# One visit for the adapter matmul pairs of a routed body's second and third tile, with the other engines' tile work in another order

## Reference

```python
x = x + tanh(g_xattn[0]) * ssm(ctx_1024, layernorm(x))      # scan over DI = 512 channels x DS = 16 states
x = x + tanh(g_ffn[0]) * moe(layernorm(x))
# ssm, per step of the scan:
state = state * exp(d_t * A) + (d_t * u_t) * B_t
y_t = einsum('ben,bn->be', state, C_t)
# moe: F = 8 experts, K = 8 sub-experts each, R = 8 (adapter rank), I = 352
def _fused_linear(x, W, qa, qb, scale, w):
    out = x @ W.T
    a = einsum('th,krh->tkr', x, qa)
    b = einsum('tkr,khr->tkh', a, qb)
    return out + scale * einsum('tkh,tk->th', b, w)
def expert(..., w):
    xe = x + w @ muW.T
    gate = silu(_fused_linear(xe, gW, gqa, gqb, gs, w))
    up = _fused_linear(xe, uW, uqa, uqb, us, w)
    return _fused_linear(gate * up, dW, dqa, dqb, ds, w)
# y = sum over experts of their output times a routing weight, plus a shared expert of width 704
```

## Time and profile before

| | us |
|---|---|
| median of 3 runs (lowest, highest) | 1700.19 (1699.39, 1701.23) |
| the profiled execution's own time | 1701.69 |
| its span, first to last instruction | 1699.9 |
| busy: TensorE, its weight loads | 1576.4 (93%), 1161.0 (68%) |
| busy: DVE, ACT, POOL | 1166.0 (69%), 617.0 (36%), 727.1 (43%) |

### The profile page before, as it was taken

How to read it: one execution, slowest core, us unless ns; L and a number is a source line. 1 busy time by engine, 2 the same in 40 slices (tenths; PEclk the granted TensorE clock), 3 DMA queues, 4 the chain that set the end, 5 groups by cost and what they waited for, 6 DMA issues and landing times.

```text
span 1699.9 us, 19507 instructions
## 1 busy us (share of the span) xinstructions
PE 1576.4 (93%) x6856; PEld 1161.0 (68%) x6856; DVE 1166.0 (69%) x1638; ACT 617.0 (36%) x971; POOL 727.1 (43%) x522
## 2 busy tenths in 40 slices
PE   3788798798889999999999999999999999999999
PEld 2434476466666678767777777777777777777776
DVE  5798864598999976488888755688888653333333
ACT  4555344444454433433433243433433221111111
POOL 2377322389798811067777401287687000000000
PEclk8799899799999999999999999999999999999999
DMA  3555735887878755757567545577665456566552
GB/s 132 155 199 191 268 108 190 273 324 279 282 279 287 264 216 190 250 204 254 204 222 257 184 160 199 182 283 235 241 243 180 151 210 218 169 225 216 199 186 84
DMA packets 109888, 365.15 MB, mean 215 GB/s; under 512 B 20000, under 2 KB 45600, under 8 KB 94048
## 3 DMA queue, kind: packets, MB, share of 16 engines
q1 hardware_dynamic: 100320, 330.09, 55.9%
q10 hardware_dynamic: 9472, 33.82, 5.8%
HBM read 293.62 MB, written 70.25 MB: 214 GB/s over the span
## 4 chain that ended last, share of the span: by engine, by line
PE 62%; DVE 21%; issue 6%; ACT 5%; DMA 3%; POOL 2%; SPq 1%; ACTq 0%; DVEq 0%; POOLq 0%
PE b_g L690 14%; PE b_u L690 13%; PE b_u L781 7%; DVE ring L1441 5%; PE b_q L781 3%; PE b_g L781 3%; PE b_q L736 3%; DVE ring L1447 3%; PE b_g L754 3%; PE b_g L721 2%; DVE tt L1415 2%; PE b_g L714 2%; DVE xx L1415 1%; PE b_d L675 1%; DVE z L1415 1%
## 5 line engine op out<-in xcount | busy, mean ns | idle before, releaser
L1338 POOL TENSOR_TENSOR ring<-du,rep 128x512 f32<-128x512 f32 x256 | 346.6, 1357 | 172.6 <-DVE du L1519 90.7
L690 PE MATMUL b_g<-xnb,gm 128*128 128x512 f32 (+1 forms) x1440 | 360.2, 399 | 6.1 <-DVE tt L1415 5.3
L690 PE MATMUL b_u<-xnb,gm 128*128 128x512 f32 (+1 forms) x1440 | 349.2, 391 | 0.0
L690 PEld LDWEIGHTS b_g<-xnb,gm 128*128 128x128 f32 (+1 forms) x1440 | 254.6, 181 | 95.9 <-issue 30.2
L1441 DVE TENSOR_TENSOR_SCAN ring<-b_a,ring 128x512 f32<-128x512 f32 x256 | 311.0, 1215 | 10.3 <-POOL ring L1338 7.0
L1347 POOL TENSOR_TENSOR yx<-yx,ring 128x512 f32<-128x512 f32 x192 | 261.2, 1361 | 130.8 <-DVE ring L1447 130.4
L690 PEld LDWEIGHTS b_u<-xnb,gm 128*128 128x128 f32 (+1 forms) x1440 | 257.4, 179 | 71.2
L1415 DVE SCALAR_TENSOR_TENSOR tt<-tt,b_g 128x512 f32<-128x512 f32 (+1 forms) x120 | 82.0, 684 | 235.8 <-ACT tt L918 235.6
L918 ACT ACTIVATE b_a<-delta,a_neg 128x512 f32<-128x512 f32 x256 | 173.4, 681 | 120.0 <-DVE ring L1441 118.8
L781 PE MATMUL b_u<-dwt,hhl 128*128 128x512 f32 (+1 forms) x720 | 187.0, 396 | 0.4 <-DVE hhl L1418 0.4
L918 ACT ACTIVATE tt<-b_g 128x512 f32<-128x512 f32 (+1 forms) x120 | 71.1, 593 | 308.7 <-PE b_u L721 281.3
(11 more groups left out here) (231 smaller groups left out, 2117.9 us busy)
## 6 DMA issues: line engine op xcount, KB each, us to landing
gm<-scr_gm SPq DMA_DIRECT2D x60, 1024.0 KB, 7.8
dwt<-scr_dw SPq DMA_DIRECT2D x30, 1536.0 KB, 6.7
rep<-bc_d ACTq DMA_DIRECT2D x64, 512.0 KB, 5.0
gm<-scr_gm SPq DMA_DIRECT2D x30, 768.0 KB, 4.5
dqt<-scr_dq SPq DMA_DIRECT2D x24, 896.0 KB, 9.1
scr_gm<-gm SPq DMA_DIRECT2D x20, 1024.0 KB, 7.3
scr_dw<-dwt SPq DMA_DIRECT2D x10, 1536.0 KB, 6.2
qat<-scr_qa SPq DMA_DIRECT2D x24, 512.0 KB, 10.5
```

Source lines behind the costliest of these rows:

```text
L690: i = mm(out_b[0:IW[m], :], w, v, start=(n == 0), stop=(n == 11 and not is_routed(s)))
L1338: v.tensor_tensor(ring[:, T % NRING], du[:, T % 4, :], rep[:, N % NREP, 0], ALU.mult).then_inc(pool_dbu, 1)
```

## The change

TensorE does up and gate of the third tile before the second tile's adapters, and then both tiles' adapter pairs one after the other. The other engines' orders follow: ScalarE does tanh of the second and third tile one after the other, behind the slot c, and what stood between them (`h_hi` of the second, `root`, `hi("gm1")`, and in e = 0 `d_u` and the first exp) goes ahead of both or behind them. VectorE does slot c before `hidden` of the second tile, and `gate_z` of the second kind too. The tiles of h1 and c change places so that they stay in order of T. Instructions are neither added nor removed.

```diff
-            return {"a": (t0, t0 + 1), "h0": (t0 + 2,), "b": (t0 + 3,), "h1": (t0 + 4,), "c": (t0 + 5,),
+            return {"a": (t0, t0 + 1), "h0": (t0 + 2,), "b": (t0 + 3,), "c": (t0 + 4,), "h1": (t0 + 5,),
                     "h2": (t0 + 6,), "d": (t0 + 7,), "e": (t0 + 8,), "f": (t0 + 9,)}[slot]
...
# TensorE, routed
                 up(s, 1, 1)
-                adapters(s, 1).then_inc(pe_gu, 1)
                 up_waits(s, 2)
                 up(s, 2, 0)
                 up(s, 2, 1)
+                adapters(s, 1).then_inc(pe_gu, 1)
                 adapters(s, 2).then_inc(pe_gu, 1)
...
# ScalarE, routed
-                tanh(s, 1)
-                slot("h1")
-                h_hi(s, 1)
                 if more and e == 0:
                     d_u(nb, range(HC))
                     exp_tile(nb, 0)
                 if more and e == 4:
                     tanh_z(nb, 1)
                 if more and e == 5:
                     tanh_z(nb, 3)
+                slot("c")
+                tanh(s, 1)
+                tanh(s, 2)
+                slot("h1")
+                h_hi(s, 1)
+                if more and e == NF - 1:
+                    root(2 * nb + 1)
+                slot("h2")
+                h_hi(s, 2)
                 if split_next:
                     hi("gm1", s + 1)
-                slot("c")
-                if more and e == NF - 1:
-                    root(2 * nb + 1)
-                tanh(s, 2)
-                slot("h2")
-                h_hi(s, 2)
...
# VectorE, routed
-                hidden(s, 1, mid("h1"))
-                slot("c")
                 if more and e == 4:
                     gate_z(nb, 1)
                 if more and e == 5:
                     gate_z(nb, 3)
+                slot("c")
+                hidden(s, 1, mid("h1"))
                 if more and e == NF - 1:
                     variances(2 * nb + 1)
                     scales(2 * nb + 1, False)
```

## The result

The changed kernel takes 1731.58 us (median of 4 runs, 1730.29 to 1733.01) against 1700.31 for the kernel before, timed beside it (4 runs, 1699.39 to 1701.23). The ratio is 1.0182, with a 95% interval of 1.0166 to 1.0198. The forecast was slower, by 15.2 us; it is slower by 31, outside the range of 1703 to 1726.

The account below looks back on a forecast made before the run. TensorE bounds b = 1 to 3, VectorE (nearly GpSimd) b = 0. Terms: b = 0 +5.6, b = 1 and 2 +11.0, b = 3 -1.4, together +15.2 on 1701.7; median 1715.4 us, range 1703 to 1726.

Parts of the forecast that it names:

- The merged visit's saving: TensorE, routed bodies: one entry and exit of the adapter visit goes in each, 0.43 us.
- The width: TensorE's step from 128-column to 96-column pairs: taken as 0.23 like others; as a mode change, 10 us worse.
- Hidden and adapter_a in b = 1 and 2: TensorE waits at adapter_a for the third tile's late hl: +1.1 in e = 2, 6; -0.25 in e = 1, 5.
- e = 4: b = 1, 2: c_copy and shared zt delay the hiddens; less a wait already there, +0.85 each.
- e = 7: No qa fills the gap, work between hiddens delays norm_x1: +3.6 in b = 1, 2, +3.0 in b = 0; b = 3 +1.6.
- b = 0, e = 1 to 6: VectorE-bound bodies: GpSimd stands at lo_piece until hi("gm1"), now behind the third tile's rounding; +4.5 in all.
- The chain from the end of VectorE's h of the third tile: b = 0, e = 1: hi ends about 376.6, piece 2.37, two tile steps of 1.3; scan input at 381.6, not 381.29.
- The next thing in GpSimd's queue: b = 0, e = 1 to 6: GpSimd work behind the scan's input, for which the forecast's sum has no term.
- The rest of the new orders in b = 0: e = 1 to 6: two gate_z back to back cost 0.75 in e = 4, 5; e = 2 gets 1.3 back.
- The rival of a jam in GpSimd: b = 0: GpSimd's delay stays from body to body, +10 and not +4.5; 1721 to 1728 us; 9%.
- e = 0: Third tile's tanh comes earlier, so TensorE reaches adapter_a sooner: -0.8 each in b = 1, 2, -1.9 in b = 0.
- The rival of the clock: Waits in e = 7 lower TensorE's clock, adding about 1.7 to 3 us each time; 1720 to 1726 us; 6%.

Follow-up runs that it names:

- experiment 6: Changed kernel, but in e = 2, 4 and 6 only c_copy stands behind the third tile's rounding on ScalarE; 1721.63 us, ratio 1.0124.
- Experiment 4: Changed kernel, but in e = 7 variances, scales (VectorE) and root (ScalarE) stand ahead of both tiles' hidden and tanh; 1729.03 us, ratio 1.0161.
- experiment 1: Changed kernel, but ScalarE rounds gm1 behind the second tile's rounding again, ahead of slot h2; 1712.6 us, ratio 1.0071.
- experiment 2: Kernel before, but ScalarE's rounding of gm1 moved behind the third tile's rounding; 1716.4 us, ratio 1.0085.
- experiment 3: Changed kernel, but in e = 0 ScalarE does both tanh ahead of the scan's first exp; 1724.34 us, ratio 1.0131.
- all_four: Changed kernel with gm1's rounding back, both tanh first in e = 0, variances, scales, root first in e = 7, c_copy behind the rounding; 1690.95 us, ratio 0.9944.

## Why the prediction was right in direction and wrong in size

**The merged visit's saving** (0.43) measured 0.35 in b = 3. The width costs nothing that shows. The Trainium skill (TensorEngine Tiling (Array Packing), Key Properties) says that changing the tiling mode, and not just the tile, drains the engine. The trace agrees so far as the step from 128 to 96 columns, 0.23 like the others, shows no gap.

**Hidden and adapter_a in b = 1 and 2** (+1.1 in e = 2 and 6, -0.25 in e = 1 and 5, +0.1 in e = 3): +1.2, -0.23, -0.03. The chain worked out from the earlier trace rows held, and experiment 6 took `c_copy`'s part away. e = 4 was put at +0.85 and measured +0.4.

**e = 7** (+3.6, +3.6, +3.0, and +1.6 in b = 3): +3.8, +3.6, +3.0, +1.7. Experiment 4 shows that 2.4 and 2.1 of it in b = 1 and 2 is the work between the two hiddens, as I had said.

**The step that failed: b = 0, e = 1 to 6**, "+0.4 in odd e, about +1.2 where c_copy holds the rounding too", +4.5 in all. Place and mechanism were right (GpSimd at `lo_piece("gm1")`), the sizes of the sum were not: experiment 1 prices the place at 19.7 us and experiment 2 at 15.0. Three terms are wrong.

- The chain from the end of VectorE's h of the third tile, over ScalarE's two roundings, GpSimd's piece and the tile step behind it, to the scan that needs that step's input. For e = 1 I added it up to 6.0 us (from 375.54, where that h ends in the kernel before, to 381.6), 0.3 more than VectorE's own work between these two points (5.75). In the changed kernel it takes 7.7 in e = 1, 3 and 5: the rounding of gm1 ends 1.7 behind h and not 1.1, the piece ends 2.9 later and not 2.4, the scan starts 3.1 later and not 2.6. So VectorE waits 1.89, and about 2.0 in the even bodies. The chain starts from VectorE's own h, so the wait does not depend on when VectorE comes there, as experiment 2 shows.
- The next thing in GpSimd's queue, which I put at nothing by stopping behind that scan: `scale("qb")` comes late with the rest and costs VectorE 1.4 to 1.7 more a body.
- The rest of the new orders in b = 0, put at about nothing (-1.3 in e = 2, +1.5 for `gate_z`): it gains 6.1.

The rival of a jam in GpSimd had the right sign and a chance of only 9%, and the result is above its range too. Its mechanism did not take place: no delay stays from body to body, for GpSimd stands idle for 3.6 to 6.4 us ahead of the piece in each of the six; and the place costs 3.3 a body and not 1.6.

**The second one: e = 0** (-0.8 each, -1.9 in b = 0). I let the second tile's hidden start 1.3 behind the end of softplus, where it had followed directly. On ScalarE the exp ahead of the tanh waits for that end too, with a table load of 1.28 ahead of it: VectorE stood 2.61. In b = 1 and 2 the clock fell behind TensorE's longer wait, and stayed up when that wait was taken away. The rival of the clock had been placed in e = 7; it cost time in e = 0, while the one fall in e = 7 (b = 2) cost none. With the tanh ahead (experiment 3) e = 0 is 1.9 better than before, more than the -0.8 forecast.

The two steps make 18.1 us of error (9.1; and 4.2, 2.4 and 2.5 for e = 0). The unchanged start takes 3.6 off and e = 3 and 4 take 1.2, the rest adds about 1: 14.5, by which the spans differ more (29.7) than forecast (15.2).

The Trainium skill (TensorE: Matmul & The Clock Gate, HAM oscillation — how this bites in real kernels) says that idle gaps between bursts of matmuls throttle the engine again. The windows of e = 0 agree. In e = 7 of b = 1, with waits of 1.25, 0.47 and 1.45, nine matmuls took 2.34: no fall there. In e = 7 of b = 2 the clock fell behind the same first two waits, and six matmuls took 2.75 and not 1.53; the next wait, for the third tile's h, took it up, and the body is as long as in four executions without a fall (98.8).

## What to carry to other kernels

When an instruction moves behind another on one engine, follow everything that waits for it down the other engine's whole queue, not just the next item. Where the chain starts from the consumer's own earlier work, add it up operation by operation and set it against the consumer's work between the same two points: here 0.3 us of lateness was forecast from a chain that came out 1.7 longer. A merge on the busiest engine that saves a few tenths of a microsecond is worth less than the orders around it: here the same time came with and without it, and single lines elsewhere were worth 5 to 20 us. Leave the old order where no independent work covers the longer chain, as in e = 7.

## What the hardware showed unasked

The same instructions with the same waits met either clock. The end of b = 3, e = 7, where TensorE waits 1.25 and then 0.47, took 32.8 us from its first visit to the end in five profiled executions with the merged visit there (the changed kernel among them) and 34.4 in four others. TensorE in the changed kernel, and then in `all_four`:

```profile
1712.49 0.93 PE L781 MATMUL b_g<-dwt,hhl 128*128 128x512 f32 x3 [1.25 <-issue]
1713.89 0.96 PE L781 MATMUL b_g<-dwt,hhl 128*128 128x512 f32 x3 [0.47 <-DVE hhl L1418]
1714.70 1.53 PE L781 MATMUL b_u<-dwt,hhl 128*128 128x512 f32 x6
```

```profile
1670.74 0.93 PE L781 MATMUL b_g<-dwt,hhl 128*128 128x512 f32 x3 [1.25 <-issue]
1672.14 1.63 PE L781 MATMUL b_g<-dwt,hhl 128*128 128x512 f32 x3 [0.47 <-DVE hhl L1425]
1673.57 2.49 PE L781 MATMUL b_u<-dwt,hhl 128*128 128x512 f32 x6
```

So after the same waits the clock falls or it does not. A fall costs 1.6 us here and nothing where a later wait takes it up (e = 7 of b = 2 above), and a forecast should carry it as a chance. What decides it was not settled.
